# A start buffer of its own for token rows, and five re-orderings, in a float32 gated cross-attention block

## The reference

```python
x = x + tanh(g_xattn) * attention(layernorm(x), ctx, Wq, Wk, Wv, Wd)
x = x + tanh(g_ffn)   * quantised_ffn(layernorm(x))

# attention: 32 query heads and 8 key/value heads of 128
queries = rope(q @ Wq.T); keys = rope(k @ Wk.T); values = v @ Wv.T
scores  = where(causal, queries @ keys.T * 128**-0.5, min)
out     = (softmax(scores) @ values) @ Wd.T
# quantised_ffn: rows are scaled and rounded to +-127, then gate, up, silu, down
```

## Time and profile before

| what | us |
|---|---|
| median of 3 runs (1571.01 to 1574.35) | 1572.49 |
| the profiled execution | 1571.81 |
| its span | 1570.0 |
| PE busy | 1483.4 (94%) |
| DVE busy | 988.2 (63%) |
| ACT busy | 537.5 (34%) |
| POOL busy | 626.7 (40%) |

### The profile page before, as it was taken

How to read it: one execution, slowest core, us unless ns; L and a number is a source line. 1 busy time by engine, 2 the same in 40 slices (tenths; PEclk the granted TensorE clock), 3 DMA queues, 4 the chain that set the end, 5 groups by cost and what they waited for, 6 DMA issues and landing times.

```text
span 1570.0 us, 19226 instructions
## 1 busy us (share of the span) xinstructions
PE 1483.4 (94%) x7475; PEld 1218.4 (78%) x7488; DVE 988.2 (63%) x1536; ACT 537.5 (34%) x829; POOL 626.7 (40%) x403
## 2 busy tenths in 40 slices
PE   7869999999999999999999999999999999967996
PEld 7858888888888888877777888888888888854553
DVE  5837565656565656575655656565656565668995
ACT  4314141414141413244332414141313132317884
POOL 2525343434343333330434434333333333115996
PEclk9989999999999999999999999999999999998999
DMA  8633122322222222226151222221212221192553
GB/s 293 199 83 88 43 80 50 77 53 75 55 74 56 75 56 73 57 72 232 40 171 39 75 42 74 43 74 43 74 43 65 52 58 32 52 269 93 190 182 140
DMA packets 193786, 142.92 MB, mean 91 GB/s; under 512 B 147744, under 2 KB 162592, under 8 KB 193312
## 3 DMA queue, kind: packets, MB, share of 16 engines
q1 hardware_dynamic: 193264, 138.54, 31.0%
q0 software_dynamic: 432, 3.15, 1.0%
HBM read 124.88 MB, written 19.92 MB: 92 GB/s over the span
## 4 chain that ended last, share of the span: by engine, by line
PE 79%; DVE 7%; ACT 4%; DMA 3%; POOL 3%; SPq 2%; issue 2%; POOLq 0%; ACTq 0%
PE psum L502 16%; PE psum L504 16%; PE psum L503 16%; PE psum L556 7%; PE psum L591 7%; PE psum L593 7%; PE psum L592 7%; POOL go L1171 2%; PE psum L565 2%; DVE stat L1243 1%; DVE sc L1540 1%; ACT xg L1041 1%; SPq L321 1%; DMA wk_raw<-in_wk_t 1%; ACT xu L1042 1%
## 5 line engine op out<-in xcount | busy, mean ns | idle before, releaser
L502 PE MATMUL psum<-xt_hi,wq_hi 128*128 128x512 f32 x1024 | 405.9, 396 | 6.2 <-DVE rot L1295 5.2
L504 PE MATMUL psum<-xt_hi,wq_lo 128*128 128x512 f32 x1024 | 400.3, 391 | 0.0
L503 PE MATMUL psum<-xt_lo,wq_hi 128*128 128x512 f32 x1024 | 399.9, 391 | 0.0
L1103 POOL TENSOR_TENSOR rot<-rot 128x1024 f32<-128x1024 f32 x64 | 153.7, 2401 | 456.8 <-DVE rot L1303 455.1
L1351 DVE TENSOR_TENSOR acc<-psum,acc 128x512 f32<-128x512 f32 x256 | 176.0, 689 | 164.5 <-PE psum L593 162.5
L1075 POOL TENSOR_TENSOR wd_lo<-wd_raw,wd_hi 128x512 fp32r<-128x512 f32 x128 | 166.0, 1305 | 233.3 <-ACT wd_hi L848 233.3
L502 PEld LDWEIGHTS psum<-xt_hi,wq_hi 128*128 128x128 f32 x1024 | 193.3, 189 | 45.7 <-DVE rot L1295 5.6
L1199 DVE TENSOR_TENSOR vw_lo<-psum,vw_hi 64x512 fp32r<-64x512 f32 x256 | 176.3, 689 | 81.6 <-ACT vw_hi L884 75.9
L504 PEld LDWEIGHTS psum<-xt_hi,wq_lo 128*128 128x128 f32 x1024 | 192.9, 188 | 40.9
L884 ACT ACTIVATE vw_hi<-psum 64x512 fp32r<-64x512 f32 x256 | 151.7, 593 | 209.2 <-PE psum L504 206.0
L503 PEld LDWEIGHTS psum<-xt_lo,wq_hi 128*128 128x128 f32 x1024 | 193.2, 189 | 38.4
(11 more groups left out here) (128 smaller groups left out, 1982.0 us busy)
## 6 DMA issues: line engine op xcount, KB each, us to landing
wq_raw<-in_wq_t SPq DMA_DIRECT2D x128, 256.0 KB, 4.6
wd_raw<-in_wd_t SPq DMA_DIRECT2D x128, 256.0 KB, 3.1
acc<-in_x SPq DMA_DIRECT2D x16, 512.0 KB, 6.5
x_scratch<-acc SPq DMA_DIRECT2D x16, 512.0 KB, 6.8
xa<-x_scratch SPq DMA_DIRECT2D x16, 512.0 KB, 3.3
xb<-x_scratch SPq DMA_DIRECT2D x16, 512.0 KB, 4.3
xn<-in_x SPq DMA_DIRECT2D x10, 512.0 KB, 4.9
wk_raw<-in_wk_t SPq DMA_DIRECT2D x4, 1024.0 KB, 8.2
```

The costliest lines, as they stand in the source:

```text
L502: pe.matmul(dst, a_hi, b_hi, start=start, stop=False)
L503: pe.matmul(dst, a_hi, b_lo, start=False, stop=False)
L504: return pe.matmul(dst, a_lo, b_hi, start=False, stop=stop)
L1103: pool.tensor_tensor(rot[:, 0, :, :], rot[:, 0, :, :], rot[:, 1, :, :], ALU.add).then_inc(rope_done, 1)
```

## The change

Six edits, by engine:

1. A buffer `xt_rows` takes the normalised tiles 0 to 3. It lies in the same memory as `xt_lo`, in the columns of tiles 4 to 7, which are written later. A tile is now written as 8 pieces of 128 columns, 1024 columns apart. DVE no longer waits for transposes there; `normalise(0)` waits for kv 3 instead, since `xt_lo` lies over the value weights. `normalise(2)` moves ahead of `key_rows(4)`, `normalise(3)` ahead of `key_rows(5)`, `lower_rows(0, 1)` ahead of `lower_kv(7, 0)`, and `key_rows(7)` ahead of `normalise(6)`.
2. SP loads kv 7 ahead of the first query weights, and the second query weights ahead of `store_kv(7)`, once all key products are done.
3. ACT copies tiles 4 to 7 of the first unit one after the other and splits the second query weights only then. It splits the first three Wd tiles ahead of the square root of the statistics.
4. POOL splits the last Wd tile of each half ahead of the last `add_turned`.
5. SP reloads `acc` in two parts, both in unit u = 2 of the second half: tiles 0 to 3 right after the load of query weights, tiles 4 to 7 after two Wd loads.
6. The rows are handed about as 8 x 128 views.

```diff
             xt_hi = sb(s, "xt_hi", [EC, HTOK], F32R)
+            with ExitStack() as over:
+                xt_rows = sb(over, "xt_rows", [EC, HTOK], F32)
             xt_lo = sb(s, "xt_lo", [EC, HTOK], F32R)
...
             if half == 0:
-                return rot[:, t % 2, :, :].rearrange("p a n -> p (a n)")
+                return xt_rows[:, :, (BT + t) * P:(BT + t + 1) * P]
...
             store_kv(3)
+            load_kv(7, whole, kv_in[7])
             load_wq(0)
-            load_kv(7, whole, kv_in[7])
             store_kv(4)
...
             store_kv(6)
+            sp.wait_ge(kv_ps, KVB)
+            load_wq(1)
             store_kv(7)
...
+            def load_again(tiles):
+                for t in tiles:
+                    sp.wait_ge(x1_store[t], 16)
+                    sp.wait_ge(part_done, TILES + t + 1)
+                    sp.dma_start(acc[:, t, :], x[HTILES + t, :, :]).then_inc(x_in[t], 16)
...
-                    if u % 2 == 0 and unit // 2 + 1 < HALVES * PAIRS and unit != UNITS:
-                        if unit >= 2:
-                            sp.wait_ge(q_done, unit)
-                        else:
-                            sp.wait_ge(kv_ps, KVB)
+                    if u % 2 == 0 and 1 < unit // 2 + 1 < HALVES * PAIRS and unit != UNITS:
+                        sp.wait_ge(q_done, unit)
                         load_wq(unit // 2 + 1)
+                    if u == 2 and half == 1:
+                        load_again(range(0, BT))
...
-                    if u == 3 and half == 1:
-                        for t in range(HTILES):
-                            sp.wait_ge(x1_store[t], 16)
-                            sp.wait_ge(part_done, TILES + t + 1)
-                            sp.dma_start(acc[:, t, :], x[HTILES + t, :, :]).then_inc(x_in[t], 16)
+                    if u == 2 and half == 1:
+                        load_again(range(BT, HTILES))
...
                 if kind == 0 and not filled:
                     copy_rows(half, 4)
+                    copy_rows(half, 5)
+                    copy_rows(half, 6)
+                    copy_rows(half, 7)
                     next_wq(unit, 0)
-                    copy_rows(half, 5)
                     next_wq(unit, 1)
-                    copy_rows(half, 6)
                     if unit:
                         split_wd(VPG * gg)
-                    copy_rows(half, 7)
...
+            for v in range(WDS):
+                split_wd(v)
             root(HTILES, slice(BT, HTILES))
             act.wait_ge(gate_in, 32)
             act.activation(gates[:, :], gates[:, :], ACT.Tanh).then_inc(gate_done, 1)
-            for v in range(WDS):
-                split_wd(v)
...
                     slot(half, u)
+                split_wd((half + 1) * GROUPS * VPG - 1)
                 add_turned((half + 1) * UNITS - 1)
-                split_wd((half + 1) * GROUPS * VPG - 1)
...
             def normalise(t):
-                if t == 2 or t == 3:
-                    dve.wait_ge(xt_ps, t - 1)
+                if t == 0:
+                    dve.wait_ge(kv_ps, VB)
```

More of the change, by code:

```diff
@@ L256, in rows_of, with split @@
         def rows_of(half, t):
+            def split(v):
+                return v.rearrange("p (c n) -> p c n", c=EC)
             if half == 0 and t >= BT:
-                return far[:, t, :]
+                return split(far[:, t, :])
             if half == 0:
-                return rot[:, t % 2, :, :].rearrange("p a n -> p (a n)")
+                return xt_rows[:, :, (BT + t) * P:(BT + t + 1) * P]
             if t == 0 or t == HTILES - 1:
-                return xn[:, :]
+                return split(xn[:, :])
             if t < 3:
-                return rot[:, t - 1, :, :].rearrange("p a n -> p (a n)")
-            return far[:, 2 * (t - 3), :]
+                return split(rot[:, t - 1, :, :].rearrange("p a n -> p (a n)"))
+            return split(far[:, 2 * (t - 3), :])
         def kv_weights(b):
@@ L445, in _ @@
                     for t in range(1, 3):
-                        sp.dma_start(rows_of(1, t), x[HTILES + t, :, :]).then_inc(xl_in[t], 16)
+                        sp.dma_start(rows_of(1, t), x[HTILES + t, :, :].rearrange("p (c n) -> p c n", c=EC)).then_inc(xl_in[t], 16)
                     load_k(GROUPS)
@@ L520, in turn_rows @@
                 for ec in range(EC):
-                    ins = pe.transpose(turn_banks(half, t)[:, ec * P:(ec + 1) * P], rows_of(half, t)[:, ec * P:(ec + 1) * P], ident)
+                    ins = pe.transpose(turn_banks(half, t)[:, ec * P:(ec + 1) * P], rows_of(half, t)[:, ec, :], ident)
                 ins.then_inc(xt_ps, 1)
@@ L1277, in normalise @@
             def normalise(t):
-                if t == 2 or t == 3:
-                    dve.wait_ge(xt_ps, t - 1)
+                if t == 0:
+                    dve.wait_ge(kv_ps, VB)
                 if t == BT:
                     dve.wait_ge(kv_ps, KVB - 1)
-                dve.tensor_scalar(rows_of(0, t), acc[:, t, :], mv[:, t, 0:1], rstd1[:, t:t + 1],
+                dve.tensor_scalar(rows_of(0, t), acc[:, t, :].rearrange("p (c n) -> p c n", c=EC), mv[:, t, 0:1], rstd1[:, t:t + 1],
                                   ALU.subtract, ALU.mult).then_inc(xn_done, 1)
@@ L1505, in _ @@
             lower_kv(6, 0, kv_lo_a)
+            normalise(2)
             key_rows(4)
             lower_rows(0, 0)
-            normalise(2)
+            normalise(3)
             key_rows(5)
+            lower_rows(0, 1)
             lower_kv(7, 0, kv_lo_a)
-            lower_rows(0, 1)
-            normalise(3)
             row_statistics(4)
@@ L1521, in _ @@
             reciprocal_root(2, slice(BT, HTILES), rstd1)
-            for t in range(BT, HTILES):
-                normalise(t)
+            normalise(4)
+            normalise(5)
             key_rows(7)
+            normalise(6)
+            normalise(7)
             dve.wait_ge(cst_in, 32)
```

## The result

The changed kernel takes 1547.3 us (median of four runs, 1545.9 to 1548.8), against 1573.4 us before. The ratio is 0.984 (95% interval 0.982 to 0.985): 26 us less. The profiled execution took 1548.8 us with a span of 1547.0 us and a mean granted clock of 0.989, against a span of 1570.0 us and 0.980, so the two traces have 23.0 us between them.

What follows compares the result with a forecast made beforehand. PE was taken as the bound, so time could come only from its idle or half-clock places. Start 14.7, half ends 9.7 and reload 6.7 sum to 31.1 us off, giving 1541 us, range 1536 to 1548.

Steps and rivals of the forecast that it cites:

- the slower rival: Long dense stretches: the granted clock falls below 1.00, at 0.95 the time is 1587 us; chance 0.02.
- The start, 14.7 us: Edits 1 to 3: 22.15 us of waits and half clock removed, less 7.4 of new waits; bounds 9 and 22.
- The large term: Start: the 11.9 us wait, with 2.3 us of half clock behind it, ends with copies first and query weights loaded earlier.
- None is over 2.7 us ... I count no half clock here.: Start: new waits are too short to count half clock; 2.3 us for it stay in the range.
- Wd tiles split ahead of the root ... so ACT is free in time.: Start: Wd tiles land at about 66, statistics are ready at 67.5 us; 1 us if they land later.
- The same 2 MB in the other order end at about 52.: Start: first query weights, now loaded behind key block 7, finish loading at about 52 us.
- The collision of `normalise(2)`: Start: it meets POOL's lo half of key block 6, ends 0.56 us behind it; kv 6 then waits 2.2 us.
- the next bound: Start: DVE's list makes PE wait 0.8 us at tile 4, 2.5 at tile 6, 0.9 at the second unit.
- The half ends, 4.85 us each: Edit 4: each half end gains 3.13 us of wait and 1.7 of half clock; sum 9.7, bounds 6 and 9.7.
- in the new order the lo part falls into the idle time: Half ends: the last Wd tile's lo part, 1.26 us, fits into POOL's 10.20 us of idle time.
- The reload, 6.7 us: Edit 5, second half: a 5.2 us wait and 1.5 us of half clock go; bounds 2 and 7.5.
- The start gives back more: Rival: key blocks are fed later, half clock comes ahead of kv 6; start gives 9 to 11, 1545 to 1547 us; chance 0.12.

Runs made afterwards that it cites:

- start_only: The changed kernel with the order at the half ends and the reload as before, so only the start is changed: 1562.5 us, ratio 0.993 to before.
- reload_whole: The changed kernel with the reload of the second half's token tiles back in one part, behind the fourth unit's Wd loads: 1552.5 us, ratio 0.987 to before.
- newton_late: The changed kernel with VectorE's root chain for half 2 moved behind the two operations that TensorE waits for: 1545.6 us, ratio 0.983 to before.
- loads_back: The changed kernel with SyncE's load order of the start as before; ScalarE still copies tiles 4 to 7 first: ratio 0.986 to before.
- both_back: The changed kernel with SyncE's and ScalarE's orders of the start both as before: ratio 0.989 to before.
- wq_later: The changed kernel with the first query weights' splits (ScalarE) and low parts (GpSimd) behind key block 7's, ScalarE's also behind tile 1's copy: 1546.4 us, ratio 0.983 to before.
- add_first: The changed kernel with GpSimd's last add of turned queries ahead of the last Wd low part again, at both half ends: 1552.5 us, ratio 0.987 to before.
- copies_back: The changed kernel with ScalarE's order of copies and splits in the first unit as before: ratio 0.984 to before.
- rows_on_act: The changed kernel with tiles 6 and 7 normalised on ScalarE, Wd splits spread, Wd low parts later, `normalise(2)` behind `key_rows(4)`: 1540.6 us, ratio 0.980 to before.

## Why the prediction was right, and by how much each step missed

Forecast: 31.1 us off, 1541 us, with a range of 1536 to 1548. It was 26 us, 1547.3, in the range, but only 0.7 us from its slow end. All three terms came out smaller than forecast: 11.6, 5.2 and 5.0 us in the runs where 14.7, 9.7 and 6.7 were summed.

*What bounds it.* Right. The long stretches did not move (588.0 and 523.1 us), and no slower clock came there; the slower rival is out.

*The start, 14.7 us.* Measured 11.6 by the runs of start_only, 10.6 to 12.5 in five traces from the first key block on. The large term was right: the 11.9 us wait hung on the query weights' split queued ahead of the copies. The new waits were 8.2 us where 7.4 were forecast (reload_whole's trace, which began on time): key block 6 1.2 (forecast 2.2), key block 7 1.7 (1.0), tile 4 2.2 (0.8), tile 6 2.1 (2.5), second unit 1.0 (0.9). Each restart costs some 0.25 us more: matmuls of a key block overlap by 0.16 us, and the first step behind a wait is 0.22 us instead of 0.12 (after, 37.79 to 38.01). So 22.15 less 8.2 leaves 13.9 where that trace has 12.5; the restarts are about half of the rest, and its other half is not traced to a cause. Three steps failed:

- "None is over 2.7 us ... I count no half clock here." Three of the five traces have a stretch of it in the start, 1.7 us each, behind waits of 2.29 (after, tile 6), 2.52 (newton_late, tile 4) and 2.97 us (start_only, key block 6). The 2.3 us kept for it in the range were a fair price.
- "Wd tiles split ahead of the root ... so ACT is free in time." ScalarE was. But the split releases GpSimd's low parts, and they ran into VectorE's root chain: 0.68 + 1.19 us instead of 0.16 + 0.22 there in reload_whole, 1.5 us straight into the wait for tile 4. Every instruction that a moved step releases counts, on the third engine too.
- "The same 2 MB in the other order end at about 52." They ended at 52.7 to 55.7. The four issues took 7.5 to 8.1 us behind the loads of key block 7, against 4.2 to 4.4 ahead of it (loads_back, both_back, as in the earlier trace rows). ScalarE waited 6.5 to 7.5 us with tile 1's copy behind. wq_later shows that this wait alone was not the limit.

The collision of `normalise(2)` was as foretold: it took 2.90 us and ended 0.54 us behind GpSimd's low part (0.56 forecast). This is the exclusive lock on the shared ports of the Trainium skill, SBUF — State Buffer, "SBUF: two separate sides", and the trace agrees. The price of a strided write was 0: `xt_rows` took 0.80 to 0.81 us, as `rot` did. That edit 1 brings nothing alone was not seen. The prediction added the 3.8 and 1.4 us to the gain one by one, though the list of VectorE behind them, which it named as "the next bound", sets the end for either buffer.

*The half ends, 4.85 us each.* By the runs of add_first both together give 5.2 us, not 9.7. At end 2 the wait of 3.13 us is gone and 4.74 us are traced against before; against add_first, whose clock stayed full, 3.2. The 1.7 us of half clock that the term adds came in two of three traces with this wait. At end 1 the gain is 2.4 us, or 3.7 where the clock of the new order stayed full. The step that failed there is "in the new order the lo part falls into the idle time". It was idle time of GpSimd, not of the lock: VectorE's root chain, which only half 1's end has, stands in it.

*The reload, 6.7 us.* 7.0 us against reload_whole in the traces. The two traces of before and after differ by 8.9, since the 2.59 us wait was followed by half clock in before and not in after. By the runs of reload_whole 5.0, the same within the error. The waits of 1.8 and 2.6 us stayed, as forecast.

*Rivals.* "The start gives back more" (9 to 11 us of start, 1545 to 1547) comes nearest in the sum and in size; its reasons came in part. The first query weights did reach ScalarE at 52.7 to 55.7. Half clock at key block 6 did not come in after (the block took 5.9 us behind its wait, the one before it 5.8), but it did in start_only, which has the same start:

```profile
51.60:54.90 3.30, 3.27 (x15) 3.28 (x16) 3.27 (x5) 1.04 (x2) 1.61 (x2) 0.50 0.94 223
```

By the prediction's own list half clock in the key blocks is a sign of being wrong. Of the other signs, the first scores came at 91.2 (reload_whole) to 95.8 us (after), not at 88 to 90; the rest is as it says.

## What to carry to other kernels

Draw up the waits that a change removes, but ask of each which list sets the end behind it; a wait that ends before another engine's bound only moves it, and two edits can each be worth nothing and 5 us together. When an instruction of GpSimd moves, lay its span over VectorE's timeline, small operations too. Time in which GpSimd alone is idle is not free time while VectorE works between SBUF tiles. And price a wait with and without half clock behind it, since the same wait had it in one execution and not in the next.

## What the runs showed of the hardware

The price of a collision is what is left of GpSimd's instruction, whatever the size of VectorE's. A multiply of 128x8 numbers took 2.35 us beside an addition of 2.39 us on GpSimd, and 0.17 us without one. VectorE instructions that read PSUM did not grow beside GpSimd: in after the low part of a token tile took 1.23 us at 57.81 us, with GpSimd at work, and the turn of the queries 1.21 us at 90.13 with it and at 82.52 without. The low part of key weights, which reads two SBUF tiles, did grow (from 1.23 us at 46.73 to 2.35 at 58.95). Not every instruction on SBUF does: four row statistics took 2.46 us at 61.23 beside GpSimd, where two took 1.28 at 37.65 without it, and a reciprocal took 0.18 us at 71.26 beside it.

TensorE's clock behind a short wait is not settled by the wait's length. Behind the same 2.6 us wait for `rot` the granted clock fell to half in 6 of the 14 traces and not in 8. First copies_back, then after (us, busy of PE, PEld, DVE, ACT, POOL, clock, DMA, GB/s):

```profile
780.70:784.20 3.50, 3.45 (x17) 3.48 (x18) 0.48 (x2) 1.51 (x3) 3.16 (x3) 0.56 0.39 146
```

```profile
783.70:787.20 3.50, 3.50 (x24) 3.20 (x25) 0.63 (x2) 1.72 (x4) 3.31 (x3) 1.00 0.41 153
```

That is 17 matmuls against 24 in the same time, and 1.6 us on the reload stretch (71.4 against 69.8). The wait of 2.67 us at end 1 did the same: 17.7 or 16.4 us. Between 20 and 1390 us the shortest wait with half clock behind it was 2.13 us (rows_on_act, at 58.25), the longest without it 3.12 us (add_first, at 1357.83); none under 2.1 us had it, and all of 3.36 us and more did. In after, the half-clock stretch behind the wait at end 1:

```profile
697.20:700.80 3.60, 3.60 (x10) 2.81 (x9) 2.51 (x5) 2.06 (x3) 2.38 (x1) 0.53 0.93 214
```

Two such places make some 3 us of difference between executions, as much as some of the edits studied here.
